# Layer 1 of a graph-network kernel: 25 instead of 24 of a chunk's 56 columns picked by matmul, in four one-hot blocks instead of three

## The chip, the cores and the metric

The kernel runs on one core of a Trainium2 chip. The metric is the device time of one execution in microseconds (us). The engines are called PE (TensorE, matmul), DVE (VectorE), ACT (ScalarE), POOL (GpSimd) and SP (SyncE, here only a queue that starts transfers).

## What is computed

Four graph-network layers follow each other over the same graph of 6,250 nodes with 32 features and 200,000 edges, sorted by their destination. The change touches the second, "layer 1", which is this:

```python
norm_h = feat / norm
cos = jnp.sum(norm_h[src] * norm_h[dst], axis=-1)
e = beta[0] * cos
m = jax.ops.segment_max(e, dst, num_segments=N)
p = jnp.exp(e - m[dst])
s = jax.ops.segment_sum(p, dst, num_segments=N)
out = jax.ops.segment_sum(feat[src] * (p / s[dst])[:, None], dst, num_segments=N)
```

So each edge needs the row of its source node (32 features and one scale, 33 numbers), and then a score, running maxima, an exponential and running sums along the sorted edges.

## The kernel before, in words

The edges stand in 128 partitions with 1,568 columns each. A layer goes through them in `NCH` = 28 chunks of `C` = 56 columns, and each column of a chunk needs 128 source rows in `G1[c % 2]`. They come in two ways:

- **Gathered.** POOL starts one indirect transfer for each of the first `C - KP` = 32 columns (L1532, `l1g<-T,srcs`). `paced(j, picks)` keeps gather j of a chunk no further ahead than four picks of its share.
- **Picked.** The last `KP` = 24 columns of a chunk are picked from the node table, which PE holds as `QS1` (`qs` in the trace), by one-hot matrices. A pick is 8 matmuls into one of three PSUM banks (L1601, `ps<-qs,l1oh`), and a `take` on DVE (L1775, TENSOR_REDUCE `l1g<-ps`) reduces that bank into the column. Pick n waits until take n-3 is done (`z1["red"]`).

The one-hots are made in blocks of `SB1` = 8 columns, so three a chunk (`NB1`). A block has four groups (`PG`). For each group DVE compares keys with a ramp (L1769, TENSOR_SCALAR `nd<-...ramp`) and ACT widens the result (`widen`, L1699, CAST `l1oh<-nd`). The narrow results have two buffers, so a group waits for the widening of the last but one. The first pick of a block waits for all four groups of it (`z1["oh"]`). The groups of the next block are made behind takes 0, 1, 2 and 3 of the present one (`SPREAD1`).

The order on each engine is written out by hand. Between the takes DVE does the arithmetic of the chunk before: `chunk(c - 1)` is a generator of which one step is done behind each take from k = 1 on. Its first step (L1816, `l1of<-l1g,psv`) waits until all gathers of that chunk have landed. Step 2 is a reduction (L1819), steps 3 and 4 are short, step 7 has L1839 and the product L1841, steps 9 and 12 are the two scans L1849. `fill(c)` prepares the present chunk behind take 19 (copies L1783 and L1785, a scan L1795) and take 21 (a second scan, copies L1799 and L1802). It waits for two copies by ACT, `lays` (L1734, `psv<-l1s`) and `fm` (L1737, `nd<-m`), in this order. ACT's order for a chunk is: widen block 1, the exponentials and `spread` (L1713), widen block 2, `lay` (two copies, L1718), the copies `lays` and `fm`, widen the block of the next chunk. In 15 of the chunks ACT also starts small loads of weights for layer 3 behind groups 1 and 3 of that last block.

PE runs its picks in a loop (`Fori`) whose body holds two chunks. The other engines have straight code.

Of the kernel before, what the change touches and what calls it, by code (L numbers as in the profile page):

```python
# [10 lines left out]
ALU = mybir.AluOpType  # L11
# [4 lines left out]
NC = 49  # L16
# [43 lines left out]
F1 = 34  # L60
SB1 = 8
NB1 = KP // SB1
SPREAD1 = ((0,), (1,), (2,), (3,), (), (), (), ())
CQ = 7
# [76 lines left out]
def program(nc, x, src, dst, ea16, ea2, ea32, eps, beta, w2, root2, bias2,  # L141
            eW, eb, pW, pb, poW, pob, lW, lb, out):
    ctx = ExitStack()
    with ctx:
# [299 lines left out]
        def ranked(r):  # L444
# [29 lines left out]
                              "nmm masks xc xt xts pq rep wide four xa ap wr px",  # L474
                   z1.over(g0=16 * (C - KP) * 14, g1=16 * (C - KP) * 14, starts=16 * NC, root=2 * NGR, tab=2, hat=NGR,
                           tabd=16, hatd=16, sl=16 * NCH, lays=NCH, fm=NCH, filled=2 * NCH, score=2 * NCH, ev=NCH, em=NCH,
                           av=NCH, spread=NCH, prod=NCH, scan=2 * NCH, lay=3 * NCH, o0=16 * 14, o1=16 * 14, lastT=2,
                           fa=1, fea=1, fb=1, feb=1, carry=2, carryT=2, kb0=KD4 * NB1 * NCH // 2,
                           kb1=KD4 * NB1 * NCH // 2, ob=PG * NB1 * NCH, oh=PG * NB1 * NCH, qd=17, pk=KP * NCH,
                           red=RED0 + KP * NCH, parts=3, ma=1, mea=1, fixed=1))  # L480

# [1038 lines left out]
        def layer1_g(e):  # L1520
            e.wait_ge(z1["hatd"], 16)
            e.indirect_dma_start(K0[:, :], None, NH, bass.IndirectOffsetOnAxis(
                ap=k0i[:, 0:1], axis=0)).then_inc(z1["k0"], 16)
            e.wait_ge(z1["tabd"], 16)
            for c in range(NCH):
                s = c % 2
                if c >= 2:
                    e.wait_ge(z1["prod"], c - 1)
                for j in range(C - KP):
                    if paced(j, KP) > 0:  # L1530
                        e.wait_ge(z1["red"], RED0 + KP * c + paced(j, KP))
# [12 lines left out]
        def layer1_sp(e):  # L1544
            def keys(m):
                if m >= NB1 * NCH:
                    return
                if m >= 2:
                    e.wait_ge(z1["ob"], PG * (m - 1))
                key_block(e, KB1[m % 2][:, :], KM1[m % 2], KQ * (m // NB1) + KQ - KP + SB1 * (m % NB1), SB1, z1[f"kb{m % 2}"])  # L1550

# [23 lines left out]
            for c in range(NCH):  # L1575
                for b in (2, 3, 4):
                    keys(NB1 * c + b)
                if c:
                    store(c - 1)
                else:  # L1580
                    e.wait_ge(z1["starts"], 16 * NC)
                    start_load(0)
                if c + 1 < NCH:
                    start_load(c + 1)
# [7 lines left out]
        def layer1_t(e):  # L1592
            def pick(i, r):
                if r % SB1 == 0:
                    e.wait_ge(z1["oh"], i * 2 * NB1 * PG + PG * (r // SB1 + 1))
                e.wait_ge(z1["red"], i * 2 * KP + RED0 + turn(r, 2 * KP))
                rows, at = OH1[r // SB1 % 2], 128 * (r % SB1)
                for g in range(PG):
# [7 lines left out]
            e.wait_ge(z1["parts"], 3)  # L1606
            with nc.Fori(0, NCH // 2, engines=[e.engine], hint_back_edge=True, head_slot={e.engine: 0}) as i:
                for r in range(2 * KP):
                    pick(i, r)
            last = O1[(NCH - 1) % 2]  # L1610
# [6 lines left out]
            e.transpose(ps[7][:, 0:33], fe[:, 2, :], ident[0:33, 0:33]).then_inc(z1["carryT"], 1)  # L1617
            e.wait_ge(z1["red"], RED0 + KP * NCH)
            weights3_t(e)
# [137 lines left out]
        def layer1_v(e, vc):  # L1757
# [1215 lines left out]
```

## Time and profile before

| | us |
|---|---|
| three runs, median (lowest, highest) | 11153.6 (11150.61, 11157.28) |
| profiled execution, first to last instruction (its span) | 11151.7 |
| layer 1, first pick to the last chunk's L1816 | 1437.4 to 2572.2 |
| PE busy over the span | 10314.4 |
| DVE busy over the span | 8123.2 |
| POOL busy over the span | 8033.1 |

The profiled execution is known by its span alone; it lies between the lowest and the highest of the three runs and 1.9 us under their median. Times in the trace are counted from the start of the span. A row of the timeline gives start, length, engine, line, operation, what is written and read, how many, and in brackets how long the engine was idle before it and what it waited for. Consecutive instructions of an engine on one line are merged into one row.

### The profile page before, as it was taken

Reading aid. Unit: us, or ns where it says so; the run is one execution under the profiler, and the core shown is the slowest. Engines: PE = TensorE matmul, PEld = TensorE weight load, DVE = VectorE, ACT = ScalarE, POOL = GpSimd, SP = SyncE. Lnnn points to the kernel's source line nnn. Section 1 sums busy time; section 2 is a strip of 40 time slices with the busy share of each in tenths; the row PEclk is TensorE's granted clock in tenths of the full one; section 3 lists DMA queues with packets and bytes.
Section 4 is the critical chain, followed back from the end, with each engine's and each line's share of the span. In section 5 each row is a group of like instructions: output and inputs, shape, how many; then the busy total and the mean of one; then the engine's idle time right before and its main releaser. Section 6 shows DMA issues by size and latency. Waiting matters only on the chain. (4 is left out here: it accounts for less than half of the span.)

```text
span 11151.7 us, 151197 instructions
## 1 busy us (share of the span) xinstructions
PE 10314.4 (92%) x54349; PEld 9851.2 (88%) x54349; DVE 8123.2 (73%) x11930; ACT 6691.2 (60%) x6650; POOL 8033.1 (72%) x8209
## 2 busy tenths in 40 slices
PE   4999579996999999998999899989999899989998
PEld 4999578885999999997999899979999899989997
DVE  4766578886999999996666666666666666666666
ACT  2444245555999999994555455555555455545554
POOL 5777777775766666664777777777777777777776
PEclk8999799997999999999999999999999999999998
DMA  7444154434333333332333333333333333333333
GB/s 239 144 128 126 54 96 99 99 99 128 88 90 89 88 91 88 88 86 74 110 107 110 96 110 110 109 99 104 110 108 105 96 110 110 108 96 110 110 110 92
DMA packets 670413, 1174.96 MB, mean 105 GB/s; under 512 B 198121, under 2 KB 456582, under 8 KB 650550
## 3 DMA queue, kind: packets, MB, share of 16 engines
q1 hardware_dynamic: 366218, 837.19, 22.8%
q0 software_dynamic: 287360, 294.17, 13.1%
q10 hardware_dynamic: 16504, 40.39, 1.2%
q14 instruction: 271, 2.22, 0.1%
q8 instruction: 60, 0.98, 0.0%
HBM read 790.81 MB, written 422.62 MB: 109 GB/s over the span
## 5 line engine op out<-in xcount | busy, mean ns | idle before, releaser
L2512 PE MATMUL ps<-qs,oh 128*128 128x416 f32 (+1 forms) x27200 | 5342.7, 351 | 124.6 <-ACT oh L2598 59.6
L2327 POOL DMA_INDIRECT l3g<-TQ,srcs x4440 | 4262.8, 960 | 1534.8 <-issue 1057.2
L2512 PEld LDWEIGHTS ps<-qs,oh 128*128 128x128 f32 x27200 | 4912.6, 188 | 401.7 <-DVE l3g L2711 210.7
L2711 DVE TENSOR_REDUCE l3g<-ps 128x32 f32<-128x416 f32 x3400 | 1920.1, 584 | 1568.3 <-PE ps L2512 1568.3
L2598 ACT CAST oh<-nd 128x1536 fp32r<-128x1536 bf16 x1140 | 1676.8, 1471 | 1722.5 <-DVE nd L2705 1722.5
L2191 PE MATMUL ps<-l2mm,l2oh 128*128 128x384 f32 (+3 forms) x12544 | 2311.6, 346 | 24.5 <-DVE l2mm L2265 24.5
L2191 PEld LDWEIGHTS ps<-l2mm,l2oh 128*128 128x128 f32 x12544 | 2279.1, 188 | 40.6 <-DVE l2mm L2265 25.3
L2175 POOL DMA_INDIRECT l2g<-Y,place x1568 | 1605.0, 1024 | 738.2 <-issue 396.4
L2265 DVE TENSOR_TENSOR l2mm<-l2hl,psv 128x1664 fp32r<-128x1664 f32 x784 | 1474.0, 1880 | 0.0
L2206 ACT ACTIVATE l2oh<-l2far,l2one 128x512 fp32r<-128x512 f16 x1568 | 1135.8, 724 | 218.3 <-PE ps L2191 45.4
L1601 PE MATMUL ps<-qs,l1oh 128*128 128x442 f32 (+1 forms) x5376 | 1060.5, 357 | 213.2 <-issue 145.6
L1601 PEld LDWEIGHTS ps<-qs,l1oh 128*128 128x128 f32 x5376 | 996.1, 189 | 277.5 <-issue 145.7
L1377 PE MATMUL ps<-qs,l0oh 128*128 128x416 f32 (+1 forms) x5824 | 1079.7, 347 | 86.6 <-ACT l0oh L1397 66.3
L1377 PEld LDWEIGHTS ps<-qs,l0oh 128*128 128x128 f32 x5824 | 1068.0, 189 | 98.3 <-issue 66.7
L2742 DVE TENSOR_TENSOR_SCAN l3of<-l3mr,psv 128x912 f32<-128x912 bf16 x560 | 1146.0, 2048 | 9.6
L2586 ACT COPY l3o<-l3of 128x1792 f32<-128x1792 f32 x280 | 994.8, 3553 | 247.0 <-DVE l3of L2742 247.0
L1303 POOL DMA_INDIRECT l0g<-T,srcs x840 | 870.5, 1036 | 339.3 <-issue 207.3
L2200 ACT ACTIVATE l2far<-l2line,nkey 128x512 f16<-128x512 f16 x1568 | 1107.9, 707 | 4.1 <-DVE l2one L2275 4.1
L1532 POOL DMA_INDIRECT l1g<-T,srcs x896 | 854.5, 954 | 273.1 <-issue 228.3
L1699 ACT CAST l1oh<-nd 128x1024 fp32r<-128x1024 bf16 x336 | 341.2, 1048 | 531.7 <-DVE nd L1769 521.7
L1451 DVE TENSOR_REDUCE l0g<-ps 128x32 f32<-128x416 f32 x728 | 420.5, 587 | 290.0 <-PE ps L1377 288.1
L2623 ACT COPY psv<-ps 128x512 f32<-128x512 f32 (+1 forms) x560 | 295.0, 527 | 500.6 <-PE ps L2501 500.6
(470 smaller groups left out, 7039.9 us busy)
## 6 DMA issues: line engine op xcount, KB each, us to landing
W<-l3o SPq DMA_DIRECT2D x140, 1792.0 KB
mneg<-KG SPq DMA_DIRECT2D x280, 384.0 KB
l3km<-KG SPq DMA_DIRECT2D x280, 360.0 KB
l3g<-TQ,srcs POOLq DMA_INDIRECT x4440
l3t<-AT SPq DMA_DIRECT2D x140, 448.0 KB, 3.9
W<-l1o SPq DMA_DIRECT2D x28, 952.0 KB, 4.1
l0e<-U_a SPq DMA_DIRECT2D x28, 896.0 KB, 4.7
S<-RX SPq DMA_DIRECT2D x49, 512.0 KB
```

The lines of the kernel that those rows point to most:

```text
L1377: x_ = e.matmul(ps[k % 4][:, 0:32 * n], OH0[k // SB0][:, g, 128 * (k % SB0):128 * (k % SB0) + 128], QS0[:, p, 32 * n0:32 * (n0 + n)], star ...
L1601: x_ = e.matmul(ps[r % 3][:, 0:F1 * n], rows[:, g, at:at + 128], QS1[:, p, F1 * n0:F1 * (n0 + n)], start=g == 0 and p == 0, stop=g == PG - ...
L2175: e.indirect_dma_start(G2[s3][:, j, :], None, cells, bass.IndirectOffsetOnAxis(ap=place[:, j0 + j:j0 + j + 1], axis=1)).then_inc(z2[f"g{s3 ...
L2191: x_ = e.matmul(ps[g][:, DG * p:DG + 32 * n], OH2[:, q % C2, 128 * g:128 * g + 128], MM[:, q % R2, p, DG * p:DG + 32 * n], start=False, st ...
L2200: e.activation(far[j % 4][:, :], line[:, :], ACT.Abs, bias=nkey[:, j:j + 1]).then_inc(z2["far"], 1)
L2206: e.activation(OH2[:, j % C2, :], far[j % 4][:, :], ACT.Relu, scale=-1.0, bias=unit[:, 0:1]).then_inc(z2["oh"], 1)
L2265: e.tensor_tensor(MM[:, r:r + 2, :, DG:MW].rearrange("p c k (h f) -> p (c k) h f", f=32), HL[u % 2][:, 2 * t:2 * t + 2, :, None, :].rearra ...
L2327: e.indirect_dma_start(G3[s][:, j, :], None, TQ, bass.IndirectOffsetOnAxis(ap=srcs[:, c * C + j:c * C + j + 1], axis=0)).then_inc(z3[f"g{s ...
L2512: x_ = e.matmul(ps[(KPX * l + k) % 3][:, 0:32 * w], OH[(l + k // SB) % 2][:, g, 128 * (k % SB):128 * (k % SB) + 128], QS[:, p, 32 * n0:32 ...
L2598: e.copy(OH[m % 2][:, g, 0:w], OB[g % 2][:, 0:w]).then_inc(z3["oh"], 1)
L2711: e.tensor_reduce(G3[i % 3][:, C - KP + k if k < KP else C - KPE + k - KP, :], ps[r % 3][:, 0:32 * PH].rearrange("p (h f) -> p f h", f=32) ...
L2742: e.tensor_tensor_scan(OF[step][:, :, :].rearrange("p f j -> p (f j)")[:, x0:x1], MR[step][:, :, :].rearrange("p f j -> p (f j)")[:, x0:x1 ...
```

## The change

Layer 1 picks `KP1` = 25 columns of a chunk and gathers 31. The one-hot blocks are 7, 6, 6 and 6 columns (`BLOCKS1`), four a chunk. `SPREAD1` keeps its four places at the start of a block. ACT widens blocks 2 and 3 of a chunk before `lay`, and the next chunk's first block behind `fm` as before. `fill` stands behind takes 20 and 22. PE's loop body holds three chunks, nine laps of it, and the 28th chunk's picks stand behind the loop as straight code. SP loads the keys of four blocks a chunk. Layers 0, 2 and 3 are untouched.

```diff
-SB1 = 8
-NB1 = KP // SB1
-SPREAD1 = ((0,), (1,), (2,), (3,), (), (), (), ())
+KP1 = 25
+BLOCKS1 = (7, 6, 6, 6)
+SB1 = BLOCKS1[0]
+NB1 = len(BLOCKS1)
+SPREAD1 = ((0,), (1,), (2,), (3,), (), (), ())
...
+def start1(m):
+    return KP1 * (m // NB1) + sum(BLOCKS1[:m % NB1])
+
+
+def place1(k):
+    b = sum(1 for x in range(1, NB1) if k >= start1(x))
+    return b, k - start1(b)
...
-                for j in range(C - KP):
-                    if paced(j, KP) > 0:
-                        e.wait_ge(z1["red"], RED0 + KP * c + paced(j, KP))
+                for j in range(C - KP1):
+                    if paced(j, KP1) > 0:
+                        e.wait_ge(z1["red"], RED0 + KP1 * c + paced(j, KP1))
...
-                for b in (2, 3, 4):
+                for b in (2, 3, 4, 5):
                     keys(NB1 * c + b)
...
-            with nc.Fori(0, NCH // 2, engines=[e.engine], hint_back_edge=True, head_slot={e.engine: 0}) as i:
-                for r in range(2 * KP):
-                    pick(i, r)
+            with nc.Fori(0, NCH // 3, engines=[e.engine], hint_back_edge=True, head_slot={e.engine: 0}) as i:
+                for d in range(3):
+                    for k in range(KP1):
+                        pick(i, d, k)
+            for k in range(KP1):
+                pick(None, NCH - 1, k)
...
-                for g in range(PG):
-                    widen(NB1 * c + 2, g)
+                for m in (2, 3):
+                    for g in range(PG):
+                        widen(NB1 * c + m, g)
                 if c:
                     lay(c - 1)
...
                 for g in range(PG):
-                    widen(NB1 * c + 3, g)
+                    widen(NB1 * c + 4, g)
...
-                for k in range(KP):
+                for k in range(KP1):
                     take(c, k)
-                    one_hots(NB1 * c + k // SB1 + 1, SPREAD1[k % SB1])
+                    b, r = place1(k)
+                    one_hots(NB1 * c + b + 1, SPREAD1[r])
                     if 1 <= k < 18:
                         next(steps, None)
-                    if k == (19 if c else KP - 1):
+                    if k == (20 if c else KP1 - 1):
                         ahead = fill(c)
                         next(ahead)
-                    if c and k == 21:
+                    if c and k == 22:
                         run(ahead)
```

Two places show how the instructions move. The first is ACT's order in one chunk, from the `spread` of the chunk before (L1713) on. Before:

```order
L1713 COPY l1ma<-l1a 128x33x56
L1699 CAST l1oh<-nd 128x1024 x4
L1718 COPY l1o<-l1of 128x56x17
L1718 COPY l1o<-l1of 128x56x16
L1734 COPY psv<-l1s 128x56x32
L1737 CAST nd<-m 128x32x56
L1699 CAST l1oh<-nd 128x1024 x2
```

The same place after the change (the line numbers are those of the changed kernel):

```order
L1733 COPY l1ma<-l1a 128x33x56
L1719 CAST l1oh<-nd 128x768 x8
L1738 COPY l1o<-l1of 128x56x17
L1738 COPY l1o<-l1of 128x56x16
L1755 COPY psv<-l1s 128x56x32
L1758 CAST nd<-m 128x32x56
L1719 CAST l1oh<-nd 128x896 x2
```

Eight widenings now stand ahead of the two copies of `lay` and of the copies `lays` and `fm`, where there were four. The second place is DVE's order around `fill`. Before, from the last group's comparison on:

```order
L1769 TENSOR_SCALAR nd<-l1kb,ramp 128x1024
L1783 COPY psv<-l1of 128x33
L1785 COPY psv<-RX 128x32
L1795 SCALAR_TENSOR_TENSOR psv<-nd,psv 128x912
L1775 TENSOR_REDUCE l1g<-ps 128x33 x2
L1795 SCALAR_TENSOR_TENSOR psv<-nd,psv 128x912
L1799 COPY RX<-psv 128x32
L1802 COPY psv<-l1of 128x32
L1775 TENSOR_REDUCE l1g<-ps 128x33 x3
```

And after the change, from the second group of the next chunk's first block on:

```order
L1791 TENSOR_SCALAR nd<-l1kb,ramp 128x896
L1805 COPY psv<-l1of 128x33
L1807 COPY psv<-RX 128x32
L1817 SCALAR_TENSOR_TENSOR psv<-nd,psv 128x912
L1797 TENSOR_REDUCE l1g<-ps 128x33
L1791 TENSOR_SCALAR nd<-l1kb,ramp 128x896
L1797 TENSOR_REDUCE l1g<-ps 128x33
L1791 TENSOR_SCALAR nd<-l1kb,ramp 128x896
L1817 SCALAR_TENSOR_TENSOR psv<-nd,psv 128x912
L1821 COPY RX<-psv 128x32
L1824 COPY psv<-l1of 128x32
L1797 TENSOR_REDUCE l1g<-ps 128x33 x3
```

Before, all four groups of the next block stood ahead of `fill`'s first scan. Now two of them stand between its two scans, and the first pick of the next chunk waits for them.

## Rows read from the trace of the kernel before

**Rows 1.** One line's instructions: ns minimum/median/maximum, first and last start, shapes

```profile
L1532 POOL DMA_INDIRECT l1g<-T,srcs x896: 940/944/1200, 1443.4 to 2569.7; - x180
...
L1816 DVE TENSOR_TENSOR l1of<-l1g,psv x28: 2020/2022/2023, 1485.0 to 2572.2; 128x1792 f32<-128x1792 f32 x28
```

**Rows 2.** Waits of DVE in 1437:2570: us in total, times, longest us

```profile
DVE l1of L1816 <- issue: 61.9, 26, 2.9
```

**Rows 3.** Timeline of PE alone, the start of two chunks and the stretch between

```profile
1892.97 35.88 PE L1601 MATMUL ps<-qs,l1oh 128*128 128x442 f32 x184 [1.02 <-DVE l1g L1775]
1930.15 1.80 PE L1601 MATMUL ps<-qs,l1oh 128*128 128x442 f32 x8 [1.30 <-DVE l1g L1775]
1932.99 35.82 PE L1601 MATMUL ps<-qs,l1oh 128*128 128x442 f32 x184 [1.03 <-DVE l1g L1775]
```

**Rows 4.** Timeline of POOL, DVE and ACT from a chunk's last gather on

```profile
1925.12 0.99 POOL L1532 DMA_INDIRECT l1g<-T,srcs  x1 [0.30 <-DVE l1g L1775]
...
1927.56 2.02 DVE L1816 TENSOR_TENSOR l1of<-l1g,psv 128x1792 f32<-128x1792 f32 x1 [2.27 <-issue]
1929.50 0.60 DVE L1775 TENSOR_REDUCE l1g<-ps 128x33 f32<-128x429 f32 x1
1930.01 0.48 DVE L1769 TENSOR_SCALAR nd<-l1kb,ramp 128x1024 bf16<-128x1024 f16 x1
...
1930.41 2.02 DVE L1819 TENSOR_REDUCE l1e<-l1of 128x56 f32<-128x1792 f32 x1
...
1932.34 0.60 DVE L1775 TENSOR_REDUCE l1g<-ps 128x33 f32<-128x429 f32 x1
...
1936.38 0.60 DVE L1775 TENSOR_REDUCE l1g<-ps 128x33 f32<-128x429 f32 x1 [0.51 <-PE ps L1601]
...
1939.86 0.60 DVE L1775 TENSOR_REDUCE l1g<-ps 128x33 f32<-128x429 f32 x1
1939.98 2.00 ACT L1699 CAST l1oh<-nd 128x1024 fp32r<-128x1024 bf16 x2 [1.10 <-DVE nd L1769]
...
1940.77 2.17 DVE L1849 TENSOR_TENSOR_SCAN l1of<-l1ma,psv 128x969 f32<-128x969 f32 x1
1942.85 0.58 DVE L1775 TENSOR_REDUCE l1g<-ps 128x33 f32<-128x429 f32 x1
```

**Rows 5.** The same timeline later in the chunk, around `lay`, `lays`, `fm` and `fill`

```profile
1945.76 3.79 ACT L1718 COPY l1o<-l1of 128x952 f32<-128x952 f32 x2
...
1949.44 1.65 ACT L1734 COPY psv<-l1s 128x1792 f32<-128x1792 f32 x1
...
1950.18 0.61 DVE L1775 TENSOR_REDUCE l1g<-ps 128x33 f32<-128x429 f32 x1 [0.93 <-PE ps L1601]
...
1951.03 1.69 ACT L1737 CAST nd<-m 128x1792 bf16<-128x1792 f32 x1
...
1955.69 0.22 DVE L1783 COPY psv<-l1of 128x33 f32<-128x33 f32 x1
...
1956.17 2.06 DVE L1795 TENSOR_TENSOR_SCAN psv<-nd,psv 128x912 f32<-128x912 bf16 x1
...
1959.15 2.05 DVE L1795 TENSOR_TENSOR_SCAN psv<-nd,psv 128x912 f32<-128x912 bf16 x1
...
1961.72 1.63 DVE L1775 TENSOR_REDUCE l1g<-ps 128x33 f32<-128x429 f32 x3
```

**Rows 6.** Comparisons and widenings at three widths: one line's instructions, ns as in Rows 1

```profile
L1445 DVE TENSOR_SCALAR l0ob<-l0kb,ramp x112: 639/654/839, 163.4 to 1244.0; 128x1664 bf16<-128x1664 f16 x112
...
L1769 DVE TENSOR_SCALAR nd<-l1kb,ramp x252: 461/478/693, 1419.9 to 2548.8; 128x1024 bf16<-128x1024 f16 x126
...
L1397 ACT CAST l0oh<-l0ob x112: 1565/1577/1609, 165.0 to 1245.4; 128x1664 fp32r<-128x1664 bf16 x112
...
L1699 ACT CAST l1oh<-nd x336: 1036/1048/1076, 1420.0 to 2549.4; 128x1024 fp32r<-128x1024 bf16 x168
```

**Rows 7.** Timeline of ACT's queue: weight loads that ACT starts in one chunk

```profile
1793.32 1.40 ACTq L1973 DMA_DIRECT2D RX<-in_L_gnn_post_W  x4
```

More of the change, by code:

```diff
@@ L474, in program @@
                               "nmm masks xc xt xts pq rep wide four xa ap wr px",
-                   z1.over(g0=16 * (C - KP) * 14, g1=16 * (C - KP) * 14, starts=16 * NC, root=2 * NGR, tab=2, hat=NGR,
+                   z1.over(g0=16 * (C - KP1) * 14, g1=16 * (C - KP1) * 14, starts=16 * NC, root=2 * NGR, tab=2, hat=NGR,
                            tabd=16, hatd=16, sl=16 * NCH, lays=NCH, fm=NCH, filled=2 * NCH, score=2 * NCH, ev=NCH, em=NCH,
@@ L478, in program @@
                            fa=1, fea=1, fb=1, feb=1, carry=2, carryT=2, kb0=KD4 * NB1 * NCH // 2,
-                           kb1=KD4 * NB1 * NCH // 2, ob=PG * NB1 * NCH, oh=PG * NB1 * NCH, qd=17, pk=KP * NCH,
-                           red=RED0 + KP * NCH, parts=3, ma=1, mea=1, fixed=1))
+                           kb1=KD4 * NB1 * NCH // 2, ob=PG * NB1 * NCH, oh=PG * NB1 * NCH, qd=17, pk=KP1 * NCH,
+                           red=RED0 + KP1 * NCH, parts=3, ma=1, mea=1, fixed=1))
         def meet(e, k):
@@ L1549, in keys @@
                     e.wait_ge(z1["ob"], PG * (m - 1))
-                key_block(e, KB1[m % 2][:, :], KM1[m % 2], KQ * (m // NB1) + KQ - KP + SB1 * (m % NB1), SB1, z1[f"kb{m % 2}"])
+                b = m % NB1
+                w = 128 * BLOCKS1[b]
+                key_block(e, KB1[b % 2][:, 0:w], KM1[b % 2][:, 0:w], KQ * (m // NB1) + KQ - KP1 + sum(BLOCKS1[:b]),
+                          BLOCKS1[b], z1[f"kb{m % 2}"])
             def start_load(c):
@@ L1592, in layer1_t, with pick @@
         def layer1_t(e):
[L1593 to L1597, printed above, removed]
+            def pick(i, d, k):
+                b, r = place1(k)
+                t, c = (0, d) if i is None else (i, d)
+                if r == 0:
+                    e.wait_ge(z1["oh"], t * (3 * NB1 * PG) + PG * (NB1 * c + b + 1))
+                e.wait_ge(z1["red"], t * (3 * KP1) + (RED0 + KP1 * c + k - 2))
+                rows, at, r = OH1[b % 2], 128 * r, KP1 * c + k
                 for g in range(PG):
@@ L1617, in layer1_t @@
             e.transpose(ps[7][:, 0:33], fe[:, 2, :], ident[0:33, 0:33]).then_inc(z1["carryT"], 1)
-            e.wait_ge(z1["red"], RED0 + KP * NCH)
+            e.wait_ge(z1["red"], RED0 + KP1 * NCH)
             weights3_t(e)
@@ L1697, in widen @@
                 if g == 0 and m >= 2:
-                    e.wait_ge(z1["pk"], SB1 * (m - 1))
-                e.copy(OH1[m % 2][:, g, :], OB1[g % 2]).then_inc(z1["oh"], 1)
+                    e.wait_ge(z1["pk"], start1(m - 1))
+                w = 128 * BLOCKS1[m % NB1]
+                e.copy(OH1[m % 2][:, g, 0:w], OB1[g % 2][:, 0:w]).then_inc(z1["oh"], 1)
             def exps(c):
@@ L1765, in one_hots @@
                     e.wait_ge(z1[f"kb{m % 2}"], KD4 * (m // 2 + 1))
+                w = 128 * BLOCKS1[m % NB1]
                 for g in groups:
@@ L1768, in one_hots @@
                         e.wait_ge(z1["oh"], PG * m + g - 1)
-                    e.tensor_scalar(OB1[g % 2], KB1[m % 2][:, :] if g else KM1[m % 2], ramp[:, g:g + 1], None, ALU.is_equal).then_inc(z1["ob"], 1)
+                    e.tensor_scalar(OB1[g % 2][:, 0:w], (KB1 if g else KM1)[m % 2][:, 0:w], ramp[:, g:g + 1], None, ALU.is_equal).then_inc(z1["ob"], 1)
             def take(c, k):
@@ L1773, in take @@
                     e.wait_ge(z1["prod"], c - 1)
-                e.wait_ge(z1["pk"], KP * c + k + 1)
-                e.tensor_reduce(G1[c % 2][:, C - KP + k, 0:33],
-                                ps[k % 3][:, 0:F1 * PH].rearrange("p (h f) -> p f h", f=F1)[:, 0:33, :],
+                e.wait_ge(z1["pk"], KP1 * c + k + 1)
+                e.tensor_reduce(G1[c % 2][:, C - KP1 + k, 0:33],
+                                ps[(KP1 * c + k) % 3][:, 0:F1 * PH].rearrange("p (h f) -> p f h", f=F1)[:, 0:33, :],
                                 AXX, ALU.max).then_inc(z1["red"], 1)
@@ L1811, in chunk @@
                 sums = V1[:, 0:32, 1:C + 1].rearrange("p f j -> p j f")
-                e.wait_ge(z1["red"], RED0 + KP * (c + 1))
-                e.wait_ge(z1[f"g{s}"], 16 * (C - KP) * (c // 2 + 1))
+                e.wait_ge(z1["red"], RED0 + KP1 * (c + 1))
+                e.wait_ge(z1[f"g{s}"], 16 * (C - KP1) * (c // 2 + 1))
                 if c:
@@ L1881, in layer1_v @@
                 steps = chunk(c - 1) if c else iter(())
-                for k in range(KP):
+                for k in range(KP1):
                     take(c, k)
-                    one_hots(NB1 * c + k // SB1 + 1, SPREAD1[k % SB1])
+                    b, r = place1(k)
+                    one_hots(NB1 * c + b + 1, SPREAD1[r])
                     if 1 <= k < 18:
                         next(steps, None)
-                    if k == (19 if c else KP - 1):
+                    if k == (20 if c else KP1 - 1):
                         ahead = fill(c)
                         next(ahead)
-                    if c and k == 21:
+                    if c and k == 22:
                         run(ahead)
```

## Prediction

> **What bounds the kernel now.** I read the line totals first, then the waits, then the timeline of one chunk. POOL starts 896 gathers from 1443.4 to 2569.7, so one each 1126.3 / 895 = 1.258 us [rows 1], and their median length of 0.94 leaves only the 0.30 that stands ahead of every one as "issue" or as a take long done. So POOL never really waits in layer 1. A chunk has 32 gathers: 32 x 1.258 = 40.27. L1816, which waits for the last gather of a chunk, comes 28 times from 1485.0 to 2572.2 [rows 1]: 1087.2 / 27 = 40.27. It waits 61.9 us in 26 chunks, 2.4 each [rows 2]. Layer 1 goes at POOL's pace.
>
> PE is close behind. Takes that wait for PE come each 0.60 + 0.93 = 1.535 us [rows 5]; that is a pick. From 1892.97 to 1932.99 PE needs 40.02 for 24 picks [rows 3], of which 24 x 1.535 = 36.84 is work and 3.18 are stalls, most of them at 1930.15 and 1932.99 [rows 3]: behind the late L1816 DVE is late with its takes, and PE has only three banks.
>
> **The change, part by part.** *POOL* loses 28 gathers: 31 x 1.258 = 39.01 a chunk, 1.26 less. That alone would be 28 x 1.258 = 35 us. *PE* gets one pick more: 25 x 1.535 = 38.38. So POOL's gain counts as far as PE's stalls stay under 0.6 us a chunk, and there is a gain at all only while they stay under 40.27 - 38.38 = 1.89. *SP* loads four blocks of keys instead of three; each has five picks (over 7 us) until it is compared, and I cost it nothing. If a load did take longer than this, DVE would wait at group 0 of a block. The question is what stalls PE once POOL doesn't. I walk one chunk with DVE, ACT and PE, in times from the start of its L1816.
>
> Costs, from start to start: take 0.51, comparison 0.40 at 1024 wide, L1816 and L1819 1.94 and 1.93, the scan 2.08 (1940.77 to 1942.85) [rows 4]; `lay` 3.68, `lays` 1.59, `fm` 1.69 until its end; the copies ahead of `fill`'s first scan 0.48, that scan 1.97, the second scan with its copies 2.57 [rows 5]. The 1.97 is its length of 2.06 less the 0.09 by which L1849's next instruction also starts early. A comparison costs (654 - 478) / 640 = 0.275 ns an element and a widening (1577 - 1048) / 640 = 0.83 ns [rows 6], so 768 wide they take 0.41 and 0.84, 896 wide 0.44 and 0.94; on DVE 0.32 and 0.36 from start to start. The two bounds for the 768 widening are 0.75 x 1.048 = 0.79 and 1.05; I take the line through the two widths. Picks 6 and 7 start at 1932.99 and 1934.53, pick 7 ends at 1936.06, and its take starts at 1936.38 [rows 3, 4]: 0.31 behind the end. Take 3 ends at 1932.94 and pick 6 starts at 1932.99: 0.05.
>
> - **Pick 6.** L1816 starts at 0 and nothing holds it now. Take 2 at 1.94, a comparison, L1819 at 2.77, take 3 at 4.70 to 5.30, pick 6 at 5.35. Take 1 waited for pick 1 and started at -0.83, so pick 1 ended at -1.14 and pick 5 at -1.14 + 4 x 1.535 = 5.00. Stall 0.35.
> - **Pick 13, the first of block 2.** Pick 7 ends at 8.42, take 7 at 8.73, a comparison, L1839, the product L1841 at 9.68 (1.93, as L1819), take 8 at 11.61, a comparison, take 9 at 12.44, a comparison, the scan at 13.27, take 10 at 15.35, the comparison of group 3 at 15.87, its widening 16.30 to 17.14, pick 13 at 17.19. Pick 12 ends at 5.35 + 7 x 1.535 = 16.10. Stall 1.09. Before, a block had 8 columns, so four picks lay between take 11 with this comparison and the pick that wants it; now two.
> - **Pick 24.** Take 16 at 17.19 + 4 x 1.535 + 0.31 = 23.64, the comparison of block 3's last group at 24.15, widened by 25.42. Only now does ACT come to `lay` (before, it came to it at 1945.76, 4.4 us ahead of take 16 at 1950.18 [rows 5]): `lay` 25.33, `lays` 29.01, `fm` 30.60 to 32.29. DVE has take 20 at 29.78, a comparison and the copies, and is at the scan at 31.17. It waits 1.15. Scan 32.32, take 21 at 34.29 to 34.89, pick 24 at 34.94. Pick 23 ends at 34.07. Stall 0.87. Before, `fm` ended at 1952.72 and the scan came at 1956.17 [rows 5].
> - **Pick 25, the next chunk's first.** Comparison of group 2 at 34.81, take 22, group 3 at 35.68; its widening 36.15 to 37.09, pick 25 at 37.14, and pick 24 ends at 36.48. Stall 0.66. These two groups stood ahead of `fill` before.
> - **Pick 26.** The second scan at 36.03, take 23 at 38.62 to 39.22, pick 26 at 39.27, pick 25 ends at 38.68. Stall 0.59. Pick 26 ends at 40.80, its take starts at 41.11, and with a comparison L1816 starts at 41.94, which closes the circle.
>
> The stalls are 0.35 + 1.09 + 0.87 + 0.66 + 0.59 = 3.56, the chunk 38.38 + 3.56 = 41.94: 1.67 more than 40.27, and 2.9 more than POOL needs. POOL will wait for the takes that pace it. Over 27 chunks: 27 x 1.67 = 45. Chunk 0 has a pick more and no chunk ahead of it; at the end the last L1816 no longer waits for a gather; these are +1.5 to +2.5 and -2 to -3, and I set them to 0.
>
> ACT's loads of weights for layer 3 stand behind groups 1 and 3 of the block that is late anyway. Four of them take 1.40 [rows 7], 0.35 each; a step of 7 takes 2.4. In ten chunks group 2's widening starts then at 36.3 instead of 35.3 and pick 25 comes 1.0 later; 0.6 of it replaces the stall of pick 26: +0.4. In five chunks a step has 8 and the next 5, some 3 us: +1.0. Together 10 x 0.4 + 5 x 1.0 = 9. Before, the same loads were hidden, since the block was wanted four picks later.
>
> Sum: 45 + 9 = +54 us. The profiled execution has a span of 11151.7, and would have 11206; its span is 1.9 under the median of the runs, so the median goes from 11153.6 to **11208**. Nothing behind layer 1 changes.
>
> **Bounds of the sum.** Each of the five stalls comes from a few short steps; if each is 0.1 us less, the loads are free, and the widening costs 0.79, the sum is 27 x (1.67 - 0.65) = +28. If each is 0.1 more, the widening costs 1.05 where it counts twice (0.4), and the loads cost twice as much, it is 27 x 2.57 + 18 = +87; both ends are unlikely together, and I take +28 to +72, 11182 to 11226, as this case's own range.
>
> **The rivals.**
>
> *POOL stays the bound (faster).* If PE's stalls are under 0.6 us a chunk, the chunk is 39.0 and the time 11153.6 - 35 = 11119. For it: POOL now sets the pace, L1816's wait of 2.4 goes away [rows 2], and with it most of the two stalls in [rows 3]. Against it: the order of ACT and DVE makes three new waits (picks 13, 24, 25), and two of three would have to be absent. It decides from stalls of 1.89 downward. 8 in 100.
>
> *The gain and the new waits cancel.* Stalls of 1.1 to 2.7 us, as when `fm` isn't late because ACT has slack that I don't see, or the comparisons of block 2 come early: 27 x (38.38 + 1.9 - 40.27) = 0, 11154, give or take 22. 8 in 100.
>
> *The longer loop is fetched anew (slower still).* The body of PE's loop grows from two chunks to three: 75 picks of 16 instructions and a wait, some 1,290, before 48 x 17 = 816. If each of the 8 taken branches cost a transfer that nothing hides, 2.44 us as from the last gather's start to L1816 [rows 4], it would be 54 + 20 = +74, 11228. The rows of before show nothing at the branches: PE's two stalls a chunk are alike in both chunks of a lap [rows 3]. 4 in 100. [...]
>
> **How the numbers follow.** 80 in 100 for the walk, 8 for POOL as the bound, 8 for cancelling, 4 for the fetch. Slower by over 0.2% (22 us, about what a measurement tells from no change) 0.84, within it 0.08, faster 0.08. The first and last case are both slower; the range takes in the walk's bounds and some of the middle: 11172 to 11228.
>
> **What would show it in the profile after.** L1816 without a wait for a gather; its 28 starts 41.9 apart, 42.3 to 43 in chunks 1 to 15. POOL waiting for takes, 3 us a chunk. PE waiting for ACT's widening at the first pick of blocks 0 and 2, over 1 us the latter, where before it waited for DVE alone. DVE waiting 1.1 us for L1737's successor ahead of `fill`'s scan. It is wrong if POOL still goes at 1.258 without a gap, or if PE's waits for ACT are missing.

## The result, and the profile after

The changed kernel takes **11204.44 us** (median of 4 runs, 11201.0 to 11207.61), the kernel before 11153.35 beside it: ratio 1.0044, 95% interval 1.0033 to 1.0056. It is 51 us slower; 54 were forecast. The profiled execution took 11207.61 with a span of 11205.9; the span of before was 11151.7. All kernels below ran beside the kernel before, which took 11153.3 to 11156.3 there; of five more runs, named in experiments 5 to 7, only the ratio is given, since the kernel before took 13926 to 14131 beside them, with pauses of several us on all engines.

POOL's gathers and L1838, the old L1816, of the changed kernel (one line's instructions, as in [rows 1]):

```profile
L1543 POOL DMA_INDIRECT l1g<-T,srcs x868: 938/945/1183, 1438.8 to 2608.7; - x174
...
L1838 DVE TENSOR_TENSOR l1of<-l1g,psv x28: 2000/2013/2020, 1482.3 to 2617.0; 128x1792 f32<-128x1792 f32 x28
```

A chunk is (2617.0 - 1482.3) / 27 = 42.03 us long, where [rows 1] gave 40.27. A gather comes every (2608.7 - 1438.8) / 867 = 1.349 us, no longer every 1.258, though one still lasts 0.945. The 61.9 us of waiting for the last gather in [rows 2] are gone: the view of L1838 names no wait at all.

The waits of PE, then of DVE, then of POOL in layer 1 of the changed kernel (us in total, times, longest us):

```profile
PE ps L1617 <- ACT l1oh L1719: 40.6, 54, 4.0
PE ps L1617 <- DVE l1g L1797: 23.5, 56, 0.8
```

```profile
DVE psv L1817 <- ACT nd L1758: 33.5, 27, 1.2
```

```profile
POOL l1g L1543 <- issue: 185.8, 603, 1.2
POOL l1g L1543 <- DVE l1g L1797: 156.6, 265, 1.8
```

PE now waits for a widening (L1719) twice a chunk, and VectorE for `fm` (L1758) once a chunk, ahead of `fill`'s scan. POOL's 265 waits for a take would be 80 us at the 0.30 that stands ahead of every gather; they are 156.6, so POOL really waits 77 us, 2.7 a chunk. The bound has moved from POOL to the ring of TensorE, VectorE and ScalarE.

PE alone, one chunk of the changed kernel and the start of the next (a row with x88 is eleven picks; a pick has eight matmuls):

```profile
2215.93 17.21 PE L1617 MATMUL ps<-qs,l1oh 128*128 128x442 f32 x88 [0.90 <-ACT l1oh L1719]
2233.73 1.81 PE L1617 MATMUL ps<-qs,l1oh 128*128 128x442 f32 x8 [0.59 <-DVE l1g L1797]
2236.04 1.80 PE L1617 MATMUL ps<-qs,l1oh 128*128 128x442 f32 x8 [0.50 <-ACT l1oh L1719]
2238.09 19.11 PE L1617 MATMUL ps<-qs,l1oh 128*128 128x442 f32 x96 [0.24 <-DVE l1g L1797]
2258.09 17.15 PE L1617 MATMUL ps<-qs,l1oh 128*128 128x442 f32 x88 [0.90 <-ACT l1oh L1719]
```

This is read from start to start, less 1.535 for each pick between. (Picks are counted from 0 in a chunk; pick 25 and pick 26 are picks 0 and 1 of the next one.) Pick 13 starts at 2215.93 and waited for ACT; eleven picks later comes pick 24, at 2233.73, which waited for a take held up by `fm` and the scan; pick 25, the next chunk's first, waited for ACT; pick 26 for the take behind the second scan; and 20.00 us after it the next pick 13 starts. The chunk is 2258.09 - 2215.93 = 42.16, and it has the stalls of the forecast in their places; the fifth, at pick 6, is too short to part the row x96 and is read from the starts of the matmuls, in the table further down.

Ahead of `fill`'s scan (the timeline of DVE, in an earlier chunk):

```profile
1557.06 2.06 DVE L1817 TENSOR_TENSOR_SCAN psv<-nd,psv 128x912 f32<-128x912 bf16 x1 [1.24 <-ACT nd L1758]
```

### The profile page after: what moved, and what is told of

Read it like the earlier page. It is cut to its first block and busy times, and to the rows that moved or that the text cites. A ratio compares the mean times of both kernels' runs of the same rounds, so it can differ in the third digit from the quotient of the medians.

```text
span 11205.9 us, 152053 instructions
## 1 busy us (share of the span) xinstructions
PE 10374.5 (93%) x54573; PEld 9888.9 (88%) x54573; DVE 8156.2 (73%) x12070; ACT 6727.6 (60%) x6762; POOL 8005.6 (71%) x8181
## 5 line engine op out<-in xcount | busy, mean ns | idle before, releaser
L1617 PE MATMUL ps<-qs,l1oh 128*128 128x442 f32 x5600 | 1116.9, 358 | 208.2 <-issue 141.9
L1617 PEld LDWEIGHTS ps<-qs,l1oh 128*128 128x128 f32 x5600 | 1032.2, 188 | 292.6 <-issue 162.2
L1543 POOL DMA_INDIRECT l1g<-T,srcs x868 | 828.8, 955 | 342.4 <-issue 185.8
L1719 ACT CAST l1oh<-nd 128x896 fp32r<-128x896 bf16 (+1 forms) x448 | 380.5, 860 | 536.7 <-DVE nd L1791 536.6
```

The source lines that it names most:

```text
L1617: x_ = e.matmul(ps[r % 3][:, 0:F1 * n], rows[:, g, at:at + 128], QS1[:, p, F1 * n0:F1 * (n0 + n)], start=g == 0 and p == 0, stop=g == PG - ...
```

## The experiments

**1. `fm` early.** Is the late `fm` a real part of the loss? Its copy on ScalarE goes ahead of `lay`, right behind the exponentials.

```diff
                     exps(c - 1)
+                    e.wait_ge(z1["filled"], 2 * c)
+                    e.copy(MF[:, :, 1:C + 1], m01[:, None, c * C:c * C + C].to_broadcast([128, 32, C])).then_inc(z1["fm"], 1)
                     spread(c - 1)
...
-                if c:
-                    e.wait_ge(z1["filled"], 2 * c)
-                e.copy(MF[:, :, 1:C + 1], m01[:, None, c * C:c * C + C].to_broadcast([128, 32, C])).then_inc(z1["fm"], 1)
+                if c == 0:
+                    e.copy(MF[:, :, 1:C + 1], m01[:, None, c * C:c * C + C].to_broadcast([128, 32, C])).then_inc(z1["fm"], 1)
```

> The changed kernel with one instruction of ACT moved: the copy fm (nd<-m) of a chunk stands behind the exponentials instead of behind lay and lays (not in chunk 0, where it stays). Theory A (three new waits by the order of ACT and DVE; the wait of fill's scan for fm is one of them): DVE's 1.2 us wait for that copy goes, pick 24 no longer stalls (0.87), and since the second scan then ends earlier pick 26 stalls less: the chunk goes from 42.1 to about 40.9, 27 x 1.15 = 31 us less than the changed kernel's 11204: about 11173. Theory B (25 picks with their takes are simply too much for PE and DVE together, wherever ACT's copies stand): 11204 within 5. Theory C (the longer loop of PE is fetched anew): 11204 within 5, PE's waits as before.

Measured: 11173.13 us (11167.39 to 11178.27), ratio 1.0017 [1.0008, 1.0026]; 31 us less than the changed kernel. The wait of DVE for `nd` is gone from its list. PE's waits, and one chunk of PE:

```profile
PE ps L1617 <- ACT l1oh L1719: 29.2, 35, 1.0
...
PE ps L1617 <- DVE l1g L1798: 10.1, 23, 4.5
```

```profile
2018.60 19.10 PE L1617 MATMUL ps<-qs,l1oh 128*128 128x442 f32 x96 [0.24 <-DVE l1g L1798]
2038.60 20.69 PE L1617 MATMUL ps<-qs,l1oh 128*128 128x442 f32 x104 [0.90 <-ACT l1oh L1719]
2059.51 5.69 PE L1617 MATMUL ps<-qs,l1oh 128*128 128x442 f32 x28 [0.22 <-DVE l1g L1798]
```

The chunk from 2018.60 to 2059.51 is 40.91 long, and the wait at pick 13 stays as it was, 0.90. From pick 13 to pick 26 it is 2059.51 - 2038.60 = 20.91, where the changed kernel takes 2238.09 - 2215.93 = 22.16: 1.25 less. A row of the view can hide gaps as short as these, so the row x104 doesn't show that PE no longer stalls in it. By the starts of the matmuls (the table further down) the stall of pick 24 is gone, that of pick 25 falls from 0.75 to 0.31, and that of pick 26 stays at 0.62; the expectation had the size right, but had pick 26 stall less and not pick 25. So `fm` behind `lay` costs 1.2 us a chunk, a part of it through the late widening of the next block.

**2. Groups 2 and 3 compared together.** Is the late last group of a block the other part?

```diff
-SPREAD1 = ((0,), (1,), (2,), (3,), (), (), ())
+SPREAD1 = ((0,), (1,), (2, 3), (), (), (), ())
```

> The changed kernel with groups 2 and 3 of a block both compared behind take 2 of the present block (SPREAD1 = 0, 1, 2 and 3), nothing else. Theory A: group 3 is compared one take earlier, ahead of the first scan of the chunk before, so that the first pick of block 2 no longer waits about 1.1 us for its widening, and the first pick of block 0 waits less: 42.1 to about 40.9 a chunk, 27 x 1.2 = 32 us less, about 11172. Theory B: the same work in another place, 11204 within 5. Theory C: 11204 within 5.

Measured: 11174.27 us (11170.16 to 11177.2), ratio 1.0019 [1.0009, 1.0028], 30 us less than the changed kernel. PE and DVE in layer 1:

```profile
PE ps L1617 <- DVE l1g L1797: 26.7, 79, 1.4
...
PE ps L1617 <- ACT l1oh L1719: 14.4, 27, 3.0
```

```profile
DVE psv L1817 <- ACT nd L1758: 13.0, 27, 0.8
```

PE's wait for ACT at pick 13 is gone; what is left there, 0.45 of a stall of 1.18, ends with a take. Since block 3 is then widened earlier, ScalarE comes to `lay` and `fm` earlier too: DVE's wait for `fm` falls from 33.5 to 13.0, and the stall of pick 24 goes here as well. Pick 6 stalls 0.69 instead of 0.35, as two comparisons now stand between takes 2 and 3. PE still waits for ACT once a chunk, at the next chunk's first pick. The chunk is (2590.1 - 1485.8) / 27 = 40.90 by L1838's starts.

**3. 24 picks in four blocks.** Is it the twenty-fifth pick or the fourth block? The kernel keeps four blocks but picks 24 columns again, so POOL has its 32 gathers back.

```diff
-KP1 = 25
-BLOCKS1 = (7, 6, 6, 6)
-SB1 = BLOCKS1[0]
+KP1 = 24
+BLOCKS1 = (6, 6, 6, 6)
+SB1 = 7
...
-                    if k == (20 if c else KP1 - 1):
+                    if k == (19 if c else KP1 - 1):
...
-                    if c and k == 22:
+                    if c and k == 21:
```

> 24 picks and 32 gathers a chunk as before, but four blocks of 6 columns with the changed kernel's order on ACT and DVE (fill behind takes 19 and 21), buffers for 7 columns. Theory A (block structure and order cost, not the pick): slower than the kernel before although the picks are the same; the walk gives 40.5 a chunk where POOL needs 40.3, so only the part above POOL's pace shows: +8 us, 11161 (range 11155 to 11175); PE waits for ACT's widenings at first picks of blocks. Theory B (the 25th pick costs): the same as before, 11153 within 3. Theory C (three chunks in the loop, 72 picks): +5 to +20.

Measured: 11172.36 us (11169.13 to 11181.35), ratio 1.0018 [1.0009, 1.0027]: 19 over before, where 8 were expected and up to 22 allowed. PE's waits in layer 1 and a chunk of it:

```profile
PE ps L1617 <- ACT l1oh L1719: 54.8, 54, 4.4
PE ps L1617 <- DVE l1g L1797: 27.9, 53, 0.8
```

```profile
2106.92 26.54 PE L1617 MATMUL ps<-qs,l1oh 128*128 128x442 f32 x136 [1.58 <-ACT l1oh L1719]
2134.14 1.81 PE L1617 MATMUL ps<-qs,l1oh 128*128 128x442 f32 x8 [0.69 <-DVE l1g L1797]
2136.25 1.80 PE L1617 MATMUL ps<-qs,l1oh 128*128 128x442 f32 x8 [0.30 <-ACT l1oh L1719]
2138.40 7.98 PE L1617 MATMUL ps<-qs,l1oh 128*128 128x442 f32 x40 [0.35 <-DVE l1g L1797]
2147.93 26.54 PE L1617 MATMUL ps<-qs,l1oh 128*128 128x442 f32 x136 [1.55 <-ACT l1oh L1719]
```

The chunk is 41.0. Its 24 picks are 36.8 of that and the stalls 4.2, though POOL (40.27) would let it go faster: four blocks make the kernel slower without any pick more. The wait of 1.58 stands at pick 6, the first of block 1, whose last group is compared behind L1838 and L1841 (at 2105.33, 1.6 us ahead of the pick). The expectation had 40.5 a chunk, 0.5 too little; its mechanism held. Four blocks of 6 aren't quite the blocks of the change: there the first has 7 columns, and pick 6 stalls 0.35 only. Against the changed kernel, one pick less gives back (by L1838's starts) 42.03 - 40.94 = 1.1, not 1.535.

**4. No loop.** TensorE's instructions as straight code, without the loop of three chunks.

```diff
-            with nc.Fori(0, NCH // 3, engines=[e.engine], hint_back_edge=True, head_slot={e.engine: 0}) as i:
-                for d in range(3):
-                    for k in range(KP1):
-                        pick(i, d, k)
-            for k in range(KP1):
-                pick(None, NCH - 1, k)
+            for c in range(NCH):
+                for k in range(KP1):
+                    pick(None, c, k)
```

> The changed kernel with PE's layer 1 as straight code, no loop at all, everything else alike. Theory A: 11204 within 4, the stalls of PE at the same picks with the same lengths. Theory C (taken branches of the longer body cost): lower by up to 20 us, and a gap less in every third chunk. Theory B: 11204 within 4.

Measured: 11205.14 us (11201.93 to 11208.91), ratio 1.0048 [1.0034, 1.0062]. Its product L1835, the counterpart of L1838:

```profile
L1835 DVE TENSOR_TENSOR l1of<-l1g,psv x28: 2001/2012/2021, 1480.7 to 2614.6; 128x1792 f32<-128x1792 f32 x28
```

(2614.6 - 1480.7) / 27 = 42.00 us a chunk, as with the loop, and the time is within the 4 us expected. The loop costs nothing that these runs can tell.

**5. One gather less in the kernel before.** From chunk 2 on, column 31 isn't gathered and keeps an older chunk's rows: a part of the computation is left out. This asks whether POOL bound the kernel before.

```diff
-                for j in range(C - KP):
+                for j in range(C - KP - (c >= 2)):
...
-                e.wait_ge(z1[f"g{s}"], 16 * (C - KP) * (c // 2 + 1))
+                e.wait_ge(z1[f"g{s}"], 16 * ((C - KP) * (c // 2 + 1) - c // 2))
```

> The kernel before with one gather left out per chunk from chunk 2 on, 26 gathers fewer; column 31 of those chunks keeps an older chunk's rows, so a part of the computation is left out. Theory A, that the issue of the gathers is the bound of layer 1 in the kernel before: its chunk of 40.27 loses one gather of 1.258, 26 x 1.258 = 33 in all, and the time comes to 11120 (11116 to 11128; a little more where TensorE's own chunk of 24 picks, some 39 by its rows, begins to show). Rival, that TensorE's or VectorE's chunk was as long as the issue already: 11153, and POOL's queue would show waits of more than 1 us for VectorE's release of the buffer in every chunk.

> The same kernel as the two runs before it of this name, both of which fell on chips where the kernel before takes 13900 or more. On a chip where it takes 11153: theory A, that the issue of the gathers bounds layer 1 of the kernel before: 26 x 1.258 = 33 less, 11120 (11116 to 11128). Rival, that TensorE's or VectorE's chunk was as long as the issue already: 11153.

The first two runs had ratios 1.0001 [0.9973, 1.0028] and 0.9978 [0.9959, 0.9996] and don't decide. The instructions were hardly longer in them (L1775 had a median of 603 ns, and 598 in the kernel before), but with the pauses between them L1816 came only every (3220.7 - 1780.9) / 27 = 53.3 us in the first, so POOL's pace bound nothing there. The third run: 11122.44 us (11119.37 to 11125.95) beside 11156.34, ratio 0.997 [0.9959, 0.9981], 34 less where 33 were expected. The gathers and L1816 of it:

```profile
L1532 POOL DMA_INDIRECT l1g<-T,srcs x870: 940/944/1256, 1443.6 to 2542.4; - x174
```

```profile
L1816 DVE TENSOR_TENSOR l1of<-l1g,psv x28: 2020/2021/2022, 1485.3 to 2544.8; 128x1792 f32<-128x1792 f32 x28
```

In the profile, the last L1816 starts 27.4 us earlier than in [rows 1], which is 26 x 1.258 = 32.7 less 5.2, since a gather's step is now (2542.4 - 1443.6) / 869 = 1.264. POOL doesn't wait more for that: it is idle 0.30 ahead of a gather as before (265.2 us ahead of 870 of them, 273.1 ahead of 896 before). The gathers themselves were longer, 0.960 us on average for 0.954; why isn't known. The profiled execution, 11125.95, was the longest of the seven, 3.5 over their median. POOL was the bound, and still is with a gather less; the rival's 11153 is refuted.

**6. Both kinds of repair together.** The changed kernel with `fm` early as in experiment 1, and the comparisons early in another way than in experiment 2: groups 0 and 1 stand behind one take, so that groups 2 and 3 come one take earlier. The second half of `fill` stands one take later.

```diff
-SPREAD1 = ((0,), (1,), (2,), (3,), (), (), ())
+SPREAD1 = ((0, 1), (2,), (3,), (), (), (), ())
...
-                    if c and k == 22:
+                    if c and k == 23:
```

> The changed kernel with three edits at once: the copy of fm right behind the exponentials, the first two groups of widenings joined in one, and VectorE's fill set behind takes 20 and 23. Theory A, that a chunk of the changed kernel is TensorE's 25 picks of 1.535 (38.4) and what the one-hots' handover adds: the two single edits took 1.2 off each chunk (40.91 and 40.9 instead of 42.1) for reasons that lie at different picks, so together a chunk is 39.5 to 39.9, which is less than the 40.3 of the kernel before, and the time is 11136 to 11145 (0.1 per cent under before). Rival, that both edits took away the same stall: 11165 to 11172. A second rival: the gathers' issue, 31 of 32 at 1.258 = 39.0 in the changed kernel, or VectorE's own chunk, is as long as 40.3: then it stays at 11153.

> The same kernel as the runs before it of this name, on a chip where the kernel before takes 11155. Theory A, that the two single edits take away different stalls: a chunk of 39.5 to 39.9 instead of 42.1, and 11136 to 11145. Rival, that both took away the same stall: 11165 to 11172. Second rival, VectorE's chunk or the issue is as long as 40.3: 11155.

The first two runs had ratios 0.9952 [0.993, 0.9973] and 0.9954 [0.9935, 0.9974]. The third: 11147.84 us (11140.5 to 11153.61) beside 11153.53, ratio 0.9994 [0.9985, 1.0003]. Its L1839 and two steps of PE:

```profile
L1839 DVE TENSOR_TENSOR l1of<-l1g,psv x28: 2009/2014/2020, 1485.5 to 2560.0; 128x1792 f32<-128x1792 f32 x28
```

```profile
2100.03 27.99 PE L1617 MATMUL ps<-qs,l1oh 128*128 128x442 f32 x144 [0.43 <-DVE l1g L1798]
2128.47 11.05 PE L1617 MATMUL ps<-qs,l1oh 128*128 128x442 f32 x56 [0.45 <-DVE l1g L1798]
2139.92 27.88 PE L1617 MATMUL ps<-qs,l1oh 128*128 128x442 f32 x144 [0.41 <-DVE l1g L1798]
```

PE has no wait for ACT any more. The chunk is (2560.0 - 1485.5) / 27 = 39.80, in the expected range, and 2.2 less than that of the changed kernel. That is near the 1.2 and 1.1 of the two single edits, but it doesn't show that they add: each of them took the stall of pick 24 away by itself, the groups are joined otherwise here, and `fill` has moved too. What the run shows is that the stalls of picks 24, 25 and 26 can all go, and that about 0.7 is left at picks 6 and 13, where PE waits for takes; none of the three edits was taken back alone. By the chunk the time should be 27 x 0.47 = 13 under before, and it is 6 under, which this measurement can't tell from nothing (where the rest is, stands below). So the expected 11136 to 11145 was missed by 3, and the first rival, 11165 to 11172, is refuted.

**7. 25 picks in three blocks.** The pick more is kept, the fourth block is not: blocks of 9, 8, 8 columns in one chunk and 8, 9, 8 in the next, so that one of the two buffers is 9 and the other 8 wide. Some small tensors move into a free part of another to make room, TensorE has straight code, and the keys of block 1 are loaded later at the start of the layer. Unlike what the expectation says, `fm` stands behind `lays` in the kernel that ran, but ahead of it ScalarE has four widenings, as in the kernel before, not eight.

```diff
-BLOCKS1 = (7, 6, 6, 6)
-SB1 = BLOCKS1[0]
-NB1 = len(BLOCKS1)
-SPREAD1 = ((0,), (1,), (2,), (3,), (), (), ())
+BLOCKS1 = ((9, 8, 8), (8, 9, 8))
+SB1 = 9
+NB1 = 3
+SIZES1 = (9, 8)
+SPREAD1 = ((0,), (1,), (2,), (3,), (), (), (), (), ())
...
-                for m in (2, 3):
-                    for g in range(PG):
-                        widen(NB1 * c + m, g)
+                for g in range(PG):
+                    widen(NB1 * c + 2, g)
...
-                    if c and k == 22:
+                    if c and k == 23:
```

> The 25 picks in three blocks of one-hots (9, 8, 8 columns in one chunk and 8, 9, 8 in the next) instead of four, with fm's copy early and the fill behind takes 20 and 23; TensorE's instructions as straight code. Blocks of 8 or 9 widenings are read for 12 or 13 us each, so neither buffer is waited for: theory A gives TensorE 25 x 1.535 and one short wait, 38.7, and the bound is again the issue of 31 gathers, 31 x 1.258 = 39.0: 27 x 1.27 = 34 less than before, 11119 (11116 to 11132). Rival, that the wider comparisons and the keys of a larger block lengthen ScalarE's or VectorE's chunk to 40 or more: 11145 to 11165.

> The same kernel as the run before it of this name, on a chip where the kernel before takes 11155. The gather less took 33 off the kernel before, so a chunk bound by the issue of 31 gathers is worth 27 x 1.258 = 34: theory A gives TensorE 38.7 and the issue 39.0, and 11120 (11117 to 11132). Rival, that the wider comparisons and the keys of a larger block lengthen ScalarE's or VectorE's chunk to 40 or more: 11145 to 11165.

The first run had a ratio of 0.9954 [0.9936, 0.9972]. The second: **11129.53 us** (11119.14 to 11132.78) beside 11153.53, ratio 0.9976 [0.9967, 0.9985], in the expected range; the rival's 11145 and more is refuted. Its L1840, POOL's waits, and a chunk of PE:

```profile
L1840 DVE TENSOR_TENSOR l1of<-l1g,psv x28: 2000/2001/2020, 1489.3 to 2545.7; 128x1792 f32<-128x1792 f32 x28
```

```profile
POOL l1g L1548 <- issue: 215.3, 704, 1.1
POOL l1g L1548 <- DVE l1g L1799: 51.0, 164, 1.3
```

```profile
2122.05 38.93 PE L1623 MATMUL ps<-qs,l1oh 128*128 128x442 f32 x200 [0.30 <-DVE l1g L1799]
```

All 25 picks of a chunk stand in one row, x200, with stalls of 0.5 in it (the table further down). The chunk is (2545.7 - 1489.3) / 27 = 39.13, next to POOL's 31 x 1.258 = 39.01, and POOL waits for takes only 51.0 - 164 x 0.30 = 2 us more than the step that stands ahead of every gather. Layer 1 starts late in it: DVE waits 18.9 us once for the keys of block 1, the first L1840 is 4.3 behind the first L1816 of [rows 1], and the last one 26.5 ahead of the last. So the pick more pays 24 us in this kernel, and in the changed one it costs 51. Not all of these 75 us are the fourth block: `fill`'s second half stands one take later here, and no run moves it alone. Experiment 6 has it there too, with four blocks and `fm` early, and takes 39.80 a chunk for 39.13 and 18 us more.

## Why the prediction was right, step by step

**The bound before.** POOL, by 1.258 a gather: shown by experiment 5, where 26 gathers less took off 34 us by the medians and 27 in the rows of layer 1; 33 were due. POOL didn't wait more with 31 gathers than with 32.

**The five stalls.** By the rows of PE after, from start to start: picks 6 and 13 together 20.00 - 12 x 1.535 = 1.58 (forecast 1.44), pick 24 17.80 - 11 x 1.535 = 0.91 (0.87), pick 25 2.31 - 1.535 = 0.77 (0.66), pick 26 2.05 - 1.535 = 0.51 (0.59). Together 3.77 for 3.56, and a chunk of 42.03 (by L1838) for 41.94. One by one, from the starts of all matmuls of layer 1 in each trace (how much later than 1.535 us behind the pick before it a pick starts, with the 0.1 that the next one adds at picks 6, 13 and 26; median of the third to the 27th chunk, us):

| | pick 6 | 13 | 24 | 25 | 26 |
|---|---|---|---|---|---|
| forecast | 0.35 | 1.09 | 0.87 | 0.66 | 0.59 |
| changed kernel | 0.35 | 1.18 | 0.76 | 0.75 | 0.62 |
| 1, `fm` early | 0.36 | 1.18 | 0.00 | 0.31 | 0.62 |
| 2, groups 2 and 3 joined | 0.69 | 0.45 | 0.01 | 0.69 | 0.66 |
| 6, both kinds | 0.74 | 0.69 | 0.00 | 0.00 | 0.01 |
| 7, three blocks | 0.50 | 0.02 | 0.01 | 0.01 | 0.02 |

Each size is within 0.11 of its forecast. The causes are shown for three places: the stall of pick 24 goes when `fm` comes early (experiment 1), and with it more than half of that of pick 25; that of pick 13 falls by 0.7 when the last group is compared one take earlier (experiment 2). The stall of pick 26 goes only in experiments 6 and 7, which both move the second half of `fill`; that this move does it is the walk's reading, not shown by a run of its own. The stall of pick 6 behind L1838 wasn't tried by itself.

**27 chunks.** 27 x (42.03 - 40.27) = 47.5, forecast 45.

**ScalarE's loads of weights, +9: this term failed.** It measured nothing. PE alone in a chunk with loads, from its pick 13 to the next:

```profile
1541.87 17.21 PE L1617 MATMUL ps<-qs,l1oh 128*128 128x442 f32 x88 [0.90 <-ACT l1oh L1719]
1559.67 1.81 PE L1617 MATMUL ps<-qs,l1oh 128*128 128x442 f32 x8 [0.59 <-DVE l1g L1797]
1561.95 1.81 PE L1617 MATMUL ps<-qs,l1oh 128*128 128x442 f32 x8 [0.47 <-ACT l1oh L1719]
...
1583.98 6.24 PE L1617 MATMUL ps<-qs,l1oh 128*128 128x442 f32 x31 [0.90 <-ACT l1oh L1719]
```

It is 42.11 long, and pick 25 comes 2.28 behind pick 24; without loads, in the chunk at 2215.93, these are 42.16 and 2.31. All chunks from the third to the 27th take 42.04 to 42.19 from first pick to first pick, with loads or without, so the 42.3 to 43 that the prediction named for chunks 1 to 15 isn't there. The same stretch (the timeline of ACT, ACTq and DVE; ACTq is ScalarE's DMA queue):

```profile
1555.01 0.45 DVE L1791 TENSOR_SCALAR nd<-l1kb,ramp 128x896 bf16<-128x896 f16 x1
1555.28 1.68 ACT L1758 CAST nd<-m 128x1792 bf16<-128x1792 f32 x1
...
1555.50 0.28 ACTq L1992 DMA_DIRECT2D pT<-in_L_gnn_pre_W  x1
...
1555.82 0.75 ACTq L1993 DMA_DIRECT2D bx<-in_L_gnn_pre_W  x1
1556.60 0.32 ACTq L1994 DMA_DIRECT2D RX<-in_L_gnn_pre_W  x1
...
1556.87 0.94 ACT L1719 CAST l1oh<-nd 128x896 fp32r<-128x896 bf16 x1
1556.95 1.05 ACTq L1996 DMA_DIRECT2D RX<-in_L_gnn_post_W  x3
...
1557.71 0.94 ACT L1719 CAST l1oh<-nd 128x896 fp32r<-128x896 bf16 x1
...
1558.03 0.52 ACTq L1996 DMA_DIRECT2D RX<-in_L_gnn_post_W  x1
...
1560.00 1.81 ACT L1719 CAST l1oh<-nd 128x896 fp32r<-128x896 bf16 x2 [1.36 <-DVE nd L1791]
```

In the program the loads stand behind group 1's widening. That widening starts at 1557.71, but the loads begin at 1555.50, right after its comparison ended at 1555.01 + 0.45 = 1555.46. Here these seven loads, which stand in ScalarE's order behind instructions whose waits were met, were issued while the engine still worked on those. The loads are through at 1558.55, and the engine waits for the next comparison until 1560.00 anyway. The prediction had put them one behind the other.

**The ends, 0.** From [rows 1] the first L1816 was at 1485.0 and the first L1838 is at 1482.3: -2.7; the last one is 44.8 later. Of the 2.7, 2.1 stood before layer 1: the last comparison of layer 0 starts at 1244.0 in [rows 6] and at 1241.9 in the changed kernel. Layer 1 as a whole is 45 us longer up to the last of them, where 54 were forecast (45 + 9 + 0).

**Nothing behind layer 1: this didn't hold in the profiles.** The profile of after ends 54.2 later than that of before, its last L1838 44.8 later. Layer 2 adds 0.8 of the 9.4 between, the start of layer 3 adds 5.1, and the rest comes little by little. The start of layer 3, PE alone, before and after:

```profile
5080.68 2.68 PE L2463 MATMUL psv<-hpb,l3of 128*128 128x256 f32 x6 [7.96 <-ACT l3of L2558]
...
5092.06 3.32 PE L2463 MATMUL psv<-hpb,l3of 128*128 128x256 f32 x8 [1.55 <-DVE RX L2684]
...
5097.36 1.76 PE L2463 MATMUL psv<-hpb,l3of 128*128 128x256 f32 x8 [1.55 <-DVE RX L2684]
...
5113.98 21.27 PE L2512 MATMUL ps<-qs,oh 128*128 128x416 f32 x116 [1.00 <-DVE qs L1147]
```

```profile
5126.29 2.69 PE L2486 MATMUL psv<-hpb,l3of 128*128 128x256 f32 x6 [8.09 <-ACT l3of L2581]
...
5142.99 3.33 PE L2486 MATMUL psv<-hpb,l3of 128*128 128x256 f32 x8 [1.55 <-DVE RX L2707]
...
5163.21 25.05 PE L2535 MATMUL ps<-qs,oh 128*128 128x416 f32 x128 [0.99 <-DVE qs L1158]
```

The instructions are the same, but from the first row to the last it is 33.30 us before and 36.92 after. The clock granted to TensorE differs: over this stretch it was 0.66 of full speed before and 0.50 after (0.50 is 1.2 GHz of 2.4). Before, it was 0.97 from 5097 to 5107, where eight matmuls take 1.76 us; after, all such groups take 3.3. In the 4 us behind the last row's start it was 1.00 before and 0.63 after, which is the rest of the 5.1. Experiment 4, whose chunks are as long as the changed kernel's, takes 33.99 us there at 0.67, and ends 48.5 later than before, not 54.2. Experiment 6 has the slow form too, 37.20 us at 0.50, and that is where its missing us are: its last L1839 is 12.2 ahead of the last L1816 of [rows 1], its end 6.6. Why the clock rose early in one execution and not in another isn't known; layer 3 is the same code in all of them, and only one execution of each kernel is profiled.

The medians are 51 apart, so if layer 1 is 44.8 longer in every execution, some 6 of the 51 lie behind it. The forecast of 54 against 51 measured is thus partly luck: the loads, 9 too many, stand against 2.5 too little in the chunks and these 6 us.

**The rivals.** POOL doesn't stay the bound, as its 77 us of real waits show; the gain and the waits don't cancel; and no run shows that the loop of three chunks is fetched anew: 11204.44 with the loop, 11205.14 without (experiment 4). The Trainium skill, page "Runtime: NRT & Kernel Launch", section "Instruction fetch mechanics", gives TensorE room for 2,048 instructions, in blocks of 256, and says that a taken branch whose target isn't in the current window of two pages waits for a fetch. The body of some 1,290 instructions is longer than two such blocks, and no wait of that kind shows in these runs. The kernel marks the loop with `hint_back_edge=True`, and no run leaves that out.

## What to carry to other kernels

Work taken from the engine that sets the pace is worth only as much as the next ring of engines has room for, and the room isn't the sum of their work (here 25 x 1.535 = 38.4 of 40.3), but that sum with its handovers. Each split of a double-buffered block into more blocks makes the time between "compared" and "needed" shorter and adds a place where the reader can wait: three blocks of 25 picks gave 24 us, and four cost 51 in the order of the change; with that order mended (experiment 6) four came to 6 under before, which can't be told from nothing. When a reader starts to wait, look for what stands in order ahead of the late instruction on the engine that makes it: here one copy, moved, gave back 31 us.

## What the runs showed of the hardware that wasn't expected

ScalarE's DMA issues ran ahead of its engine: seven loads were issued from 1555.50 to 1558.55, the first of them 2.2 us before the engine started the widening (1557.71) that stands ahead of them in the program; of their 3.05 us nothing lay on the path. The same short matmuls at the start of layer 3 took 33.3 us in one execution and 36.9 in another, by the clock that was granted (0.66 and 0.50), in code that the change doesn't touch. And a body of TensorE's loop half as long again, some 1,290 instructions, cost nothing that these runs can tell: 42.03 us a chunk with the loop, 42.00 without.
